# Two node units in every three ticks under the first gathers, and ScalarE normalising their second layer by rows

## What is computed

```python
h = jnp.maximum(_layernorm(x, axis=-1), 0.0)
x = x + relu(relu((h + segment_sum(relu(h[src]), dst)) @ W1 + b1) @ W2 + b2)
h = jnp.maximum(_layernorm(x, axis=-1), 0.0)
x = x + _L1_gnn_ref(h, edge_index, edge_attr_64, edge_weight, ...)   # V = h @ Wv + bv; K, Q, three hops over the edges
```

## The kernel before

| ticks after t | VectorE | ScalarE | TensorE |
|---|---|---|---|
| -1 | | square of x, L658 | |
| 0 | sums of x and of its square, L1153 | | |
| 1 | z = x normalised, L1132 and L1134 | | turn z, L762 |
| 2 | | copy with relu, L587 | product W1, L853 |
| 3 | | relu with bias, L597 | product W2, L770 |
| 4 | x1 = x + relu(product), L1176 | square of x1, L631 | |
| 5 | sums of x1 and its square, L1150 | | |
| 6 | h1 = x1 normalised, L1139 and L1141 | | turn h1, L762 |
| 7 | | copy with relu, L592 | product Wv, L770 |
| 8 | output rows, L1171 | | |

## Time and profile before

### The profile page before, as it was taken

One profiled execution on the slowest core, in us unless ns is written; L12 is line 12 of the kernel. 1 busy time (PEld: TensorE's weight loads), 2 busy tenths in 40 slices (PEclk: granted clock), 3 DMA queues, 4 the chain that ended last, 5 costly groups with the idle time before them and its releaser, 6 DMA issues. The chain is left out here.

```text
span 1812.7 us, 22165 instructions
## 1 busy us (share of the span) xinstructions
PE 1345.3 (74%) x5794; PEld 840.3 (46%) x5794; DVE 1488.8 (82%) x3207; ACT 1015.2 (56%) x2815; POOL 1193.0 (66%) x1185
## 2 busy tenths in 40 slices
PE   3666778788888985777777277778577898877772
PEld 3455666665666664454544033333233344455551
DVE  5866777789989886799999799999456788699992
ACT  4556878768878875455554255555355556333330
POOL 7775666616665531777773577777477777777776
PEclk9787898879978877798998589888799999988886
DMA  4394333334655554699998588888435554466650
GB/s 126 77 51 123 102 104 102 91 94 132 149 134 141 133 135 92 213 323 319 320 318 293 177 288 305 307 309 299 152 98 159 146 160 135 128 174 175 173 152 17
DMA packets 280787, 313.83 MB, mean 173 GB/s; under 512 B 168577, under 2 KB 198137, under 8 KB 268118
## 3 DMA queue, kind: packets, MB, share of 16 engines
q1 hardware_dynamic: 223734, 246.39, 45.3%
q0 software_dynamic: 56928, 66.04, 14.6%
HBM read 214.54 MB, written 161.32 MB: 207 GB/s over the span
## 5 line engine op out<-in xcount | busy, mean ns | idle before, releaser
L924 PE MATMUL bank<-product,ident 128*128 128x512 f32 (+1 forms) x800 | 383.3, 637 | 134.9 <-DVE product L1278 134.9
L533 POOL DMA_INDIRECT state<-state_hop,slot_of_src x392 | 395.6, 1009 | 126.1 <-issue 108.5
L703 ACT ACTIVATE bank<-state,norm 128x512 f32<-128x512 f32 x392 | 251.1, 679 | 254.9 <-DMA state<-state_hop,slot_of_src 221.6
L1278 DVE TENSOR_TENSOR product<-bank,queries 128x512 f32<-128x512 f32 x392 | 261.2, 687 | 90.0 <-ACT bank L703 88.3
L924 PEld LDWEIGHTS bank<-product,ident 128*128 128x128 f32 x800 | 160.9, 206 | 356.0 <-issue 182.7
L495 POOL DMA_INDIRECT x_edges<-in_x,dst_tiles x196 | 199.5, 1018 | 156.9 <-DVE x_edges L1188 97.0
L509 POOL DMA_INDIRECT row_of_src<-node_rows,pos_int x196 | 195.2, 996 | 122.2 <-DMA node_rows<-row_new 62.8
L495 POOL DMA_INDIRECT x_edges<-in_x,src_tiles x196 | 203.1, 1036 | 95.8 <-issue 54.4
L549 POOL DMA_INDIRECT out<-rows,dst_out x196 | 193.1, 985 | 59.7 <-issue 50.0
L831 PE MATMUL bank<-dst_steps,from_here 128*128 128x197 f32 x392 | 98.6, 406 | 101.7 <-ACT row_no L645 75.2
L1276 DVE SCALAR_TENSOR_TENSOR acc<-acc,same_as_before,bank 128x512 f32<-128x512 f32 x196 | 145.2, 741 | 15.9 <-ACT bank L703 15.1
(11 more groups left out here) (220 smaller groups left out, 3033.0 us busy)
## 6 DMA issues: line engine op xcount, KB each, us to landing
state_hop<-acc SPq DMA_DIRECT2D x98, 1024.0 KB, 4.7
x_nodes<-in_x SPq DMA_DIRECT2D x49, 256.0 KB, 3.6
src_row<-in_src_row SPq DMA_DIRECT2D x49, 256.0 KB, 3.6
out<-out_rows SPq DMA_DIRECT2D x49, 256.0 KB
dst_row<-in_dst_row SPq DMA_DIRECT2D x49, 256.0 KB, 4.5
kv_rows<-kv SPq DMA_DIRECT2D x49, 256.0 KB, 3.5
gg<-head_sums SPq DMA_DIRECT2D x98, 128.0 KB
kv_back<-kv_rows SPq DMA_DIRECT2D x49, 256.0 KB
```

The source lines that it names most:

```text
L533: pool.indirect_dma_start(out=mg[u % 4][:, k, :], out_offset=None, in_=d_m[hop - 1], in_offset=bass.IndirectOffsetOnAxis(ap=sidx[:, t:t + ...
L703: act.activation(pw[t % len(pw)][:, :], mg[u % 4][:, k, :], ACT.Copy, scale=wn12[:, t:t + 1]).then_inc(weighted, 1)
L924: ins = ten.matmul(ph[:, 0:k * D].rearrange("p (c j) -> p c j", j=HD), ident[:, :], part, start=(r == 0), stop=(r == HD - 1))
L1278: vec.tensor_tensor(ihj(pr[m % 2][:, u % 2 * EH + k, :]), ihj(pw[t % len(pw)][:, :]), over_j(Q[:, t, :]), ALU.mult).then_inc(multiplied, 1)
```

## The change

Two of every three ticks start a node unit in the first phase (`t % 3 != 1`), 32 units in all; the other 17 start in the second phase, most of them three ticks apart. The statistics get separate columns for x and x1, since one tick may now have both. The second normalisation (h1) of the units of the first phase goes to ScalarE, one row of 64 at a time, eight instructions for a unit; the other 17 stay on VectorE. They are turned into another PSUM bank in the first phase. ScalarE's root and its search counts move to the front of its tick, behind the copies; the search is read one tick later. VectorE's x1 moves ahead of the sums. The destination compare becomes one TENSOR_TENSOR of 512 behind the statistics. The two-column DMA is cut into 28 pieces of 7 columns, one for each of ticks 12 to 39.

```diff
-DENSE_TICKS = [2 * k for k in range(1, DU + 1)]
+DENSE_TICKS = [t for t in range(2, B0 + 1) if t % 3 != 1]
+for t in range(B0 + 2, C0):
+    if t - DENSE_TICKS[-1] >= (2 if t < B0 + 10 else 3) and (t - 5 <= B0 or t - 5 not in DENSE_TICKS):
+        DENSE_TICKS.append(t)
+DENSE_TICKS = DENSE_TICKS[0:DU]
+TAIL = 7
+TAIL_AT = {12 + i: i * TAIL for i in range(T // TAIL)}
...
# SyncE
-                if g == 12:
+                if g in TAIL_AT:
+                    c = slice(TAIL_AT[g], TAIL_AT[g] + TAIL)
                     sync.wait_ge(tail_set, 2)
-                    sync.dma_start(by_slot(d_tab)[:, :, D:TW], tail[:, :, :]).then_inc(tail_kept, 16)
+                    sync.dma_start(by_slot(d_tab)[:, c, D:TW], tail[:, c, :]).then_inc(tail_kept, 16)
...
# ScalarE, ahead of the normalisations of the tick (both blocks stood behind them)
+                if g in STAT_NO:
+                    lo, hi = stats_at(g)
+                    act.wait_ge(varred, STAT_NO[g] + 1)
+                    act.activation(q[:, 3, lo:hi], q[:, 2, lo:hi], ACT.Sqrt, bias=epsc[:, 0:1],
+                                   scale=1.0 / (D * D)).then_inc(rooted, 1)
+                u = g - 3
+                if 0 <= u < CU:
+                    act.wait_ge(searched, u + 1)
...
+                m = DENSE_AT.get(g - 6)
+                if m is not None and m < LATE:
+                    wait(act, turned2_d, m - 1)
+                    normalise(qp, HT, HT, lambda k: h1d[m % 2][:, k, :],
+                              lambda k: x1d[m % R1][:, 0, k, :]).then_inc(h1_d, 1)
...
# VectorE
                 m = DENSE_AT.get(g - 6)
-                if m is not None:
+                if m is not None and m >= LATE:
...
+                u = g - S0
+                if 0 <= u < AU:
+                    vec.tensor_tensor(sel[u % 2][:, :].rearrange("p (k c) -> p k c", c=P),
+                                      drow[u % 3][:, :].rearrange("p (k c) -> p k c", c=P),
+                                      tmf[:, u * EH:(u + 1) * EH].unsqueeze(2).to_broadcast([P, EH, P]),
+                                      ALU.is_equal).then_inc(s_set, 1)
```

More of the change, by code:

```diff
@@ L47 @@
 RT = 5
-RX = 4
+RX = 5
+R1 = 4
 NR = 12
-COLS = HT + 2 * EH
+E1, E2 = 2 * HT, 2 * HT + EH
+COLS = 2 * HT + 2 * EH
 B0 = AU
@@ L61 @@
 END = max(F_STEP)
-DENSE_TICKS = [2 * k for k in range(1, DU + 1)]
-assert len(DENSE_TICKS) == DU and all(t % 2 == 0 for t in DENSE_TICKS)
+DENSE_TICKS = [t for t in range(2, B0 + 1) if t % 3 != 1]
[3 more added lines that the diff above has]
+DENSE_TICKS = DENSE_TICKS[0:DU]
+assert len(DENSE_TICKS) == DU
+TAIL = 7
+TAIL_AT = {12 + i: i * TAIL for i in range(T // TAIL)}
 DENSE_AT = {t: m for m, t in enumerate(DENSE_TICKS)}
@@ L270, in gnn, with turn2_bank @@
         ptd, pad_, pbd, pvd = bank[0:4]
+        def turn2_bank(m):
+            return bank[7] if DENSE_TICKS[m] <= B0 else ptd
+        LATE = len([t for t in DENSE_TICKS if t <= B0])
         pte, pae, pbe = bank[4], bank[5], bank[7]
@@ L750, in _, with turn_dense @@
         def _(ten):
-            turned = {1: 0, 2: 0}
             def bias(which, n):
                 return b3[:, which * P:(which + 1) * P].unsqueeze(1).to_broadcast([3, n, P])
-            def turn_dense(which, what, done):
-                wait(ten, copied1_d, turned[1])
-                wait(ten, copied2_d, turned[2])
+            def turn_dense(p, what, done):
                 for k in range(HT // 2):
-                    ins = ten.transpose(ptd[:, k * P:(k + 1) * P], what[:, 2 * k:2 * k + 2, :], ident[:, :])
+                    ins = ten.transpose(p[:, k * P:(k + 1) * P], what[:, 2 * k:2 * k + 2, :], ident[:, :])
                 ins.then_inc(done, 1)
-                turned[which] += 1
             def rows_out(p, lhs, w, which, n, done):
@@ L781, in _ @@
                     wait(ten, x1_e, u)
+                    if u == 0:
+                        ten.wait_ge(copied2_d, LATE)
                     rows_out(pbe, a1e, W2, 0, EH // 2, mm2_e)
@@ L825, in _ @@
                     ins.then_inc(fixes, 1)
-                u = g - 2
-                if 0 <= u < CU:
-                    ten.wait_ge(g_set, u + 1)
-                    wait(ten, counted, u)
-                    for k in range(EH):
-                        ins = ten.matmul(pair[:, 256 * k:256 * k + T + 1], gsel[u % 2][:, k * P:(k + 1) * P], delta[:, :],
-                                         start=True, stop=True, skip_group_check=True)
-                    ins.then_inc(searched, 1)
                 if g == B0 + 3:
@@ L858, in _ @@
                     rows_out(pbd, a1d, W2, 0, HT // 2, mm2_d)
+                u = g - 2
+                if 0 <= u < CU:
+                    ten.wait_ge(g_set, u + 1)
+                    wait(ten, counted, u)
+                    for k in range(EH):
+                        ins = ten.matmul(pair[:, 256 * k:256 * k + T + 1], gsel[u % 2][:, k * P:(k + 1) * P], delta[:, :],
+                                         start=True, stop=True, skip_group_check=True)
+                    ins.then_inc(searched, 1)
                 m = DENSE_AT.get(g - 6)
@@ L861, in _ @@
                     ten.wait_ge(h1_d, m + 1)
-                    turn_dense(2, h1d[m % 2], turned2_d)
+                    if m == 0:
+                        ten.wait_ge(prep_v, 3)
+                    if m >= LATE:
+                        wait(ten, copied1_d, len([t for t in DENSE_TICKS if t + 1 < g]))
+                    wait(ten, copied2_d, m)
+                    turn_dense(turn2_bank(m), h1d[m % 2], turned2_d)
                 m = DENSE_AT.get(g - 1)
@@ L865, in _ @@
                     ten.wait_ge(normed_d, m + 1)
-                    turn_dense(1, zd[m % 2], turned1_d)
+                    wait(ten, copied1_d, m)
+                    late = len([t for t in DENSE_TICKS if t + 6 < g])
+                    if late > LATE:
+                        wait(ten, copied2_d, late)
+                    turn_dense(ptd, zd[m % 2], turned1_d)
                 if g == 6:
@@ L1135, in _ @@
                 m = DENSE_AT.get(g - 6)
-                if m is not None:
+                if m is not None and m >= LATE:
                     vec.wait_ge(scaled, STAT_NO[g - 1] + 1)
                     wait(vec, turned2_d, m - 1)
-                    own.add(vec.tensor_tensor(h1d[m % 2][:, :, :], x1d[m % RX][:, 0, :, :], each_row(qp[:, 4, 0:HT]), ALU.mult))
+                    own.add(vec.tensor_tensor(h1d[m % 2][:, :, :], x1d[m % R1][:, 0, :, :], each_row(qp[:, 4, HT:E1]), ALU.mult))
                     own.sync()
-                    vec.tensor_tensor(h1d[m % 2][:, :, :], h1d[m % 2][:, :, :], each_row(qp[:, 5, 0:HT]), ALU.add).then_inc(h1_d, 1)
+                    vec.tensor_tensor(h1d[m % 2][:, :, :], h1d[m % 2][:, :, :], each_row(qp[:, 5, HT:E1]), ALU.add).then_inc(h1_d, 1)
+                m = DENSE_AT.get(g - 4)
+                if m is not None:
+                    vec.wait_ge(mm2_d, m + 1)
+                    wait(vec, res_d, m - R1 + 1)
+                    vec.scalar_tensor_tensor(flat(x1d[m % R1][:, 0, :, :]), pbd[:, :], 0.0, flat(xn[m % RX][:, 0, :, :]),
+                                             ALU.max, ALU.add).then_inc(x1_d, 1)
                 if g in STAT_NO:
@@ L1170, in _ @@
                     wait(vec, out_kept[m % 2], landed(m - 2, m % 2, 2))
-                    vec.tensor_tensor(flat(rd[m % 2][:, :, :]), pvd[:, :], flat(x1d[m % RX][:, 0, :, :]), ALU.add).then_inc(res_d, 1)
-                m = DENSE_AT.get(g - 4)
-                if m is not None:
-                    vec.wait_ge(mm2_d, m + 1)
-                    wait(vec, res_d, m - RX + 1)
-                    vec.scalar_tensor_tensor(flat(x1d[m % RX][:, 0, :, :]), pbd[:, :], 0.0, flat(xn[m % RX][:, 0, :, :]),
-                                             ALU.max, ALU.add).then_inc(x1_d, 1)
+                    vec.tensor_tensor(flat(rd[m % 2][:, :, :]), pvd[:, :], flat(x1d[m % R1][:, 0, :, :]), ALU.add).then_inc(res_d, 1)
                 u = g - 1
```

75 lines of the change are left out of this document (24 added, 51 removed).

## The result

The changed kernel takes **1910.1 us** (median of four runs, 1906.6 to 1917.9) against 1818.9 for the kernel before on the same chip: ratio **1.051, 95% interval 1.045 to 1.057**. The forecast was 1870, slower, with a range up to 1910. Its profiled span is 1909.7 us against 1812.7, so +97 where the sum gave +54. The direction and the main loop were read rightly; the sum was 43 us too small, for reasons that lie outside that loop.

The account below looks back on a forecast made before the run. The prediction took a root-to-root loop between ScalarE and VectorE as the bound: +71 first phase, -13 second, -4 behind tick 98, +54 us on 1815.6, so 1870, slower; range 1835 to 1910.

Parts of the forecast that it names:

- What bounds it: First phase: loop root, ScalarE's rows, squares, VectorE's sums, variance, next root sets ticks of 9.05, 7.52, 9.03 us; chance .78.
- The DMA: First phase: cutting the two-column DMA into 28 pieces removes a stall worth about 18 us.
- h1 by rows: First-phase ScalarE: eight short rows take 2.66 us a unit, nearly twice the 1.38 of two long instructions on VectorE.
- hidden chain: Rivals: root never waits; first phase only, 7.1 us a tick, total 1813, chance .09; both phases, 1786, chance .06.
- the rival had 49: First phase: TensorE sets the pace, ScalarE's wait for turned rows doubles, +49 us, total 1919; chance .07.
- the root's wait: Sign, first phase: ScalarE's root waits for the variance 1.3 to 1.9 us in nearly every tick.
- both programs have the same loads and preparation: Up to tick 9: loads and preparation are unchanged by the change, so they add no time.
- the root chain is exposed once or twice: Up to tick 9: one h1 of 2.66 and the chain of 2.48 us add +5.
- The term of 4 us for the tile ends: Ticks 52 to 54: uncovered exchange of tile ends adds about 4 us, between 0 and 8.
- the 5.24 of the third: Ticks 61 to 98: the one tick in three without a node square takes 5.24 us.
- the low clock as a rival: First phase: TensorE's low granted clock eats a 1.1 us margin for turned rows, +49 us; chance .07.
- VectorE's sum becomes the bound: Second phase: chain hidden in both phases, VectorE bounds at 5.4 us a tick instead of 6.14, total 1786; chance .06.

Follow-up runs that it names:

- e2: Changed kernel with h1 on VectorE for all units, early root kept: 1.002 of the kernel before (kind B), ticks 9 to 49 in 282.9 us.
- e12: Changed kernel with only VectorE's output rows moved ahead of x1 and the sums: 1.037 of the kernel before (kind B), ticks 9 to 49 in 341.2 us.
- e8: Changed kernel with the two preparation matmuls of tick 6 ahead of the search in TensorE's queue: 1.041 of the kernel before (kind A).
- e6: Changed kernel with only ScalarE's root moved back behind the normalisations, search left early: 1.021 of the kernel before (kind A).
- e16: Repeat of the changed kernel with only the root moved back late: 1.026 of the kernel before (kind A), ticks 61 to 98 in 198.9 us.
- e13: Changed kernel with VectorE's x1 behind the variance again from tick 61 on: 1.032 of the kernel before (kind B), ticks 61 to 98 in 231.1 us.
- e17: Changed kernel with late root, h1 on VectorE, output rows early and preparation matmuls first: 1769.6 us, .971 of the kernel before (kind A).
- e5: The changed kernel run again without edits: 1.044 of the kernel before (kind A).
- e14: Changed kernel with late root, h1 on VectorE, output rows early and preparation matmuls first, on kind B: .989 of the kernel before.

## Why the prediction was off

**Right.** *What bounds it.* The loop from root through ScalarE's rows to the squares and VectorE's sums. Ticks in the first phase were forecast at 9.05, 7.52 and 9.03, and are 9.0, 9.07 and 7.5 where nothing else disturbs; e2 took h1 out of it and got the computed 282. *The DMA.* No 20 us stall (the tick up to mark 17, 26.0 us before, took 7.5); 18 forecast, 20 and 22 measured on kind B. *h1 by rows.* 65 us. *The rivals.* No hidden chain with the early root in either phase, and TensorE does not set the first phase: by e12 it takes 6 us of it, where the rival had 49. ScalarE's wait for turned rows did not double (48.6 us to 740 us before, 29.2 in ticks 9 to 49 now); the 5.7 and 6.8 us of that rival stand on no row. Of the forecast's signs the root's wait was too strong: it came in 27 ticks, not nearly all, and with 1.25 us on average, not 1.3 to 1.9, since in the short tick the turn of z comes last. *Luck.* A tick's sum is right to .03 because two errors of .1 cancel, as shown above. The forecast also took rows of unlike length to show the price of a TENSOR_TENSOR against a TENSOR_SCALAR; of 512 elements each, the changed kernel has .69 (L1180) and .47 (L1193).

**To tick 9, +5 forecast, +15.6 measured.** The step "both programs have the same loads and preparation" failed. The loads are the same, but TensorE's queue puts the preparation behind a search that the early root holds back. 6.5 of it is shown by e8. The rest goes with "the root chain is exposed once or twice": against before, e8 is longer by 2.5, 2.4, 2.5 and 1.6 us in ticks 5, 6, 8 and 9. With the root late, all of it is gone (e6, e16).

**Ticks 9 to 49, +66 against +72.3.** The loop itself came out. Missing was the one bank of Wv, with turns behind it, 6 us by e12, each time behind a tick at a clock of 0.55 or 0.56. Its signs stand in the order ahead of the run: two starts in consecutive ticks, and L1188 behind L1175.

**Ticks 49 to 61, 82 forecast, 89.5 measured.** The term of 4 us for the tile ends was too small: tick 55 alone took 13.2 where 7.6 stood beside it, 5.6 more. Tick 59 took 8.2 where 5.1 was forecast, with x1 2.83 late for TensorE, which was busy all through it at a granted clock of 0.51:

```profile
515.42 0.69 DVE L1152 SCALAR_TENSOR_TENSOR x_nodes<-bank,x_nodes 128x512 f32<-128x512 f32 x1 [2.83 <-PE bank L786]
```

No run changed this stretch alone, so how it divides stays open.

**Ticks 61 to 98, 227 forecast, 239.4 measured.** The computed ticks of 6.60 are there (6.62, 6.64). The term that failed is the 5.24 of the third, up to 6.9, by the move of x1, which the sum priced at nothing: e13 gives 231.1. It costs where the granted clock is 0.50 to 0.54, six ticks of 1.65 us each, 10 of the 12 us; the forecast had the low clock as a rival in the first phase only. The merged compare shows no wait of its own, but was not tried alone. The rival "VectorE's sum becomes the bound" priced 5.4 a tick rightly; it was given to the wrong kernel, since it takes the late root (5.4 a tick in e6, e16 and e17).

**Hops, +4.** Same program and same busy time of VectorE (917). From the first gather to the end of the span, e5 to e8, e16 and e17 take 1096.6 to 1105.8 us on kind A, so 1094.2 and 1098.1 differ by less than such executions do.

Common to the misses: I walked the loop over ScalarE and VectorE, and treated TensorE as a supplier with slack. Of the 43 us short (+97 against +54) some 6.5 (e8), 6 (e12) and 8 to 11 (e13, on the other kind of chip) are shown to be its queue; of the 7.5 in ticks 49 to 61, the 3.1 of tick 59 are likely so, and the tile ends are the rest.

## What to carry to other kernels

Walk a schedule's loop through every engine whose queue is in order, and through every buffer that exists once: here a single PSUM bank, read behind the variance, was enough to make a second loop that cost 43 to 47 us. Undo half of a move only with the order that it belongs to. Short row instructions move work to another engine at twice the price (2.65 against 1.38 us), and on a loop it all counts; cutting a DMA of 25,088 rows of 8 bytes into pieces was a gain of 1.1% that needed nothing else. And look at the granted clock tick by tick, not as a mean: here x1, put ahead of the sums, cost nothing in most rounds and 1.65 us where TensorE, which feeds it, stood at half its clock.

## What the runs showed of the hardware

**Two kinds of chips.** The same best kernel in the hops, on kind B (e14), beside e17's last row above on kind A:

```profile
730.00:2056.00 1326.00, 879.99 (x2684) 474.54 (x2683) 922.92 (x1781) 515.83 (x1201) 791.58 (x789) 0.77 0.56 177
```

VectorE is nearly as busy (923 against 917; this row begins 13 us ahead of the first gather, at 743.3), GpSimd too, but from the first gather the hops take 1313 us instead of 1104, with a clock of 0.77 instead of 0.85 and 177 GB/s instead of 212. Kind B also reaches tick 9 later: 116.8 in e14 against 80.7 in e17; tick 5 makes 30 of these 36 us, with 35.3 against 5.4. ScalarE's wait in it, 31.3 us, is again put down to "remote". Every trace of kind B has such waits and none of kind A; what they are is open. A change can be worth 2.9% on one and 1.1% on the other, so ratios across them are not to be mixed.

**The clock moves with the schedule.** 0.97 in a stretch of 199 us and 0.80 to 0.83 in one of 239 to 242 (kind A), with the same matmuls and only the root in another place. Tick by tick it stands at 0.50 in some rounds of the changed kernel and at 0.90 to 1.00 in others, and at 0.50 a round is 1.65 us longer where VectorE waits for what TensorE does more slowly. I had taken TensorE's 0.84 of the earlier trace rows as given, save for one rival.
